# Sixteen-chunk FFN kernel: all hidden sums kept (29 batches in DRAM, three on chip) in place of two recomputed batches, with two sets of accumulator banks

## The reference

```
x  = x + layernorm(x) * scan(ctx*ctx)        # r = 0.9*r + kv_t over the tokens
z  = layernorm(x)
zq = clip(round(z/s1), 0, 255)*s1            # s1 = max of z over ALL batches / 255
h  = relu(zq @ w1q.T + b1q)                  # w1q: int8 per row, 2048 hidden features
hq = clip(round(h/s2), 0, 255)*s2            # s2 = max of h over ALL batches / 255
x  = x + hq @ w2q.T + b2q                    # w2q: int8 per row
```

## Time and profile before

| | us |
|---|---|
| median of 3 runs | 1323.02 |
| the profiled execution, its own time | 1323.59 |
| span of the profile | 1321.8 |
| stage A, to the first quantized x2 | 0 to 353 |
| stage B, first products | 359 to 832 |
| scales | 832 to 838 |
| stage C, second products | 839 to 1316 |
| last sums out and stored | 1316 to 1322 |

### The profile page before, as it was taken

How to read it: one execution, slowest core, us unless ns; L and a number is a source line. 1 busy time by engine, 2 the same in 40 slices (tenths; PEclk the granted TensorE clock), 3 DMA queues, 4 the chain that set the end, 5 groups by cost and what they waited for, 6 DMA issues and landing times.

```text
span 1321.8 us, 17311 instructions
## 1 busy us (share of the span) xinstructions
PE 1254.0 (95%) x5514; PEld 576.9 (44%) x5514; DVE 936.5 (71%) x1348; ACT 961.1 (73%) x1355; POOL 290.8 (22%) x777
## 2 busy tenths in 40 slices
PE   6778999999599999999999999899999999999998
PEld 3333444343344444444444444344444444444443
DVE  4979999999577777777777777664565555555565
ACT  5687878787677775777657776678878857888771
POOL 2859999999500000000000000000000000000000
PEclk9888999999799999999999999899999999999999
DMA  9887999997489996999969993799999999999973
GB/s 357 325 317 262 346 332 349 335 335 283 191 316 362 347 357 237 359 350 358 363 234 349 354 353 148 271 357 416 415 415 415 415 414 364 416 415 414 415 232 128
DMA packets 131521, 443.48 MB, mean 336 GB/s; under 512 B 10340, under 2 KB 10360, under 8 KB 118904
## 3 DMA queue, kind: packets, MB, share of 16 engines
q1 hardware_dynamic: 78648, 262.18, 50.8%
q10 hardware_dynamic: 52800, 180.37, 38.4%
HBM read 257.96 MB, written 184.55 MB: 335 GB/s over the span
## 4 chain that ended last, share of the span: by engine, by line
PE 66%; POOL 17%; DMA 6%; issue 4%; DVE 4%; ACT 2%; POOLq 1%; SPq 0%; ACTq 0%; DVEq 0%
PE ps L887 35%; PE ps L944 26%; DMA out_dram<-work 4%; PE ps L912 2%; POOL rstd L448 2%; POOL pw L432 2%; PE ps L866 2%; POOL pw L434 2%; POOL pw L431 1%; DMA work<-x_scratch 1%; POOL pw L429 1%; POOL rstd L466 1%; POOL zrow L446 1%; POOL mean L427 1%; POOL pw L428 1%
## 5 line engine op out<-in xcount | busy, mean ns | idle before, releaser
L887 PE MATMUL ps<-xq,w1T 128*128 128x512 f16 x2176 | 482.2, 381 | 1.4 <-DVE xq L748 1.4
L944 PE MATMUL ps<-w2T,xq 128*128 128x512 f16 x1984 | 438.8, 381 | 5.9 <-DVE work L790 3.2
L620 ACT ACTIVATE xq<-xq,hb,hs 128x512 f16<-128x512 f32 x480 | 355.7, 804 | 104.1 <-PE ps L944 93.3
L739 DVE TENSOR_REDUCE work<-xq 128x2 f32<-128x1024 f32 x240 | 292.8, 1220 | 122.1 <-ACT xq L566 122.1
L566 ACT ACTIVATE xq<-ps 128x1024 f32<-128x1024 f32 x240 | 245.8, 1024 | 135.5 <-PE ps L887 135.2
L887 PEld LDWEIGHTS ps<-xq,w1T 128*128 128x128 f16 x2176 | 212.2, 98 | 252.9 <-issue 3.6
L866 PE MATMUL ps<-xq,work 128*128 128x512 f32 x640 | 290.7, 612 | 31.6 <-ACT xq L499 21.2
L944 PEld LDWEIGHTS ps<-w2T,xq 128*128 128x128 f16 x1984 | 193.6, 98 | 246.1 <-DVE work L790 7.2
L866 PEld LDWEIGHTS ps<-xq,work 128*128 128x128 f32 x640 | 122.6, 195 | 197.4 <-issue 147.2
L790 DVE TENSOR_TENSOR work<-ps,cs_bc 128x512 f32<-128x512 f32 x128 | 87.9, 690 | 51.6 <-PE ps L944 44.8
L499 ACT ACTIVATE xq<-ps,rstd 128x512 f32<-128x512 f32 x128 | 77.9, 689 | 62.7 <-POOL rstd L466 56.1
(11 more groups left out here) (107 smaller groups left out, 639.6 us busy)
## 6 DMA issues: line engine op xcount, KB each, us to landing
hidden_scratch<-xq SPq DMA_DIRECT2D x224, 512.0 KB, 5.8
xq<-hidden_scratch ACTq DMA_DIRECT2D x224, 512.0 KB, 10.3
work<-x_scratch SPq DMA_DIRECT2D x33, 1024.0 KB, 7.9
xq<-in_x_dram SPq DMA_DIRECT2D x32, 1024.0 KB, 8.2
x_scratch<-xq SPq DMA_DIRECT2D x32, 1024.0 KB, 5.8
xq<-in_ctx_dram ACTq DMA_DIRECT2D x31, 1024.0 KB, 5.6
out_dram<-work SPq DMA_DIRECT2D x31, 1024.0 KB, 14.7
work<-x_scratch ACTq DMA_DIRECT2D x29, 1024.0 KB, 7.2
```

What stands on the lines that cost most here:

```text
L620: act.activation(hq[c % HQ], src[:, c % 2, :], ACT.Relu, bias=hb[:, q:q + 1], scale=hs[:, q:q + 1]).then_inc(h_scaled, 1)
L739: dve.tensor_reduce(hmax[:, b * NF + 2 * q:b * NF + 2 * q + 2], src, AX.X, ALU.max).then_inc(done, 1)
L887: last = pe.matmul(bank, w1T[:, k, f * P:(f + 1) * P], xq_rows(b, k), start=(k == 0), stop=(k == KD - 1))
L944: last = pe.matmul(acc_bank(i), src[:, i * P:(i + 1) * P], w2T[:, q, :], start=first, stop=final)
```

## The change

- `RECOMPUTED` goes away. Turns are the held batches, then the stored ones. Batches 9 and 20 are copied and have their maximum taken from the copy like all others. One of the two adds to the stored batches (29), one to the held ones (`HELD = 3`).
- `NKEEP` is 6 instead of 8. The places for hidden sums on chip are 30: 6 store buffers and 24 of the held batches; all 30 take loads in stage C.
- The first loads (6, not 8) are issued by SP, as soon as the last store has landed and the last stored pair has its maximum, while PE still makes the held batches. Before, ACT issued them after the last copy.
- Two sets of four accumulator banks, used by turns: 0, 1, 6, 7 and 2, 3, 4, 5. PE waits for `scale_out` of turn s-2.
- Slots of x2 follow from the three batches that are kept there from stage B on; the order store, load, store is the same.

```diff
-RECOMPUTED = (9, 20)
-HELD = 2
+HELD = 3
 NXQ = 3
-NKEEP = 8
+NKEEP = 6
...
+        def out_slot(s):
+
+            return (NB - HELD + s) % 3
...
+        def acc_bank(s, i):
+            return ps[:, ((0, 1, 6, 7), (2, 3, 4, 5))[s % 2][i], :]
...
             def load_x2c(s):
-                sp.wait_ge(out_stored[s % 3], 16 * (s // 3))
-                sp.dma_start(x2c[s % 3].rearrange("p i d -> p (i d)"), x2_dram[turns_c[s]]).then_inc(x2c_loaded[s % 3], 16)
+                if stores_until(s) > 1:
+                    sp.wait_ge(out_stored[out_slot(s)], 16 * (stores_until(s) - 1))
+                else:
+                    sp.wait_ge(x_scaled, (NB - 2) * NI)
+                sp.dma_start(x2c[out_slot(s)].rearrange("p i d -> p (i d)"), x2_dram[turns_c[s]]).then_inc(x2c_loaded[out_slot(s)], 16)
...
+            for n in range(NKEEP):
+                sp.wait_ge(h_stored[n], 16 * stores_in(n))
+            sp.wait_ge(kept_maxed, NLOAD)
+            for c in range(NKEEP):
+                sp.dma_start(hload[c].rearrange("p n t -> p (n t)"), h_dram[c // NP2, c % NP2]).then_inc(h_loaded[c], 16)
...
             def load_kept(c):
-                if c < NKEEP:
-                    act.wait_ge(kept_maxed, NLOAD)
-                else:
-                    act.wait_ge(h_scaled, 2 * (c - NKEEP + 2 + 1))
+                act.wait_ge(h_scaled, 2 * (c - NKEEP + 1))
...
-            for c in range(NKEEP):
-                load_kept(c)
...
-            def round_fresh(g, f):
-                if f >= 8 and g == 0:
-                    dve.wait_ge(h_scaled, 4)
...
-            def fresh_chunk(g, f):
-                c = g * NF + f
...
                 if first:
-                    wait_count(pe, acc_read, (s - 1) * NI + i + 1)
-                src = fresh_hq[q] if fresh else hq[ring_chunk(s, q) % HQ]
-                last = pe.matmul(acc_bank(i), src[:, i * P:(i + 1) * P], w2T[:, q, :], start=first, stop=final)
+                    wait_count(pe, acc_read, (s - 2) * NI + i + 1)
+                if (s, i, q) == (1, 0, 0):
+                    pe.wait_ge(out_scales, 1)
+                src = hq[(s * NF + q) % HQ]
+                last = pe.matmul(acc_bank(s, i), src[:, i * P:(i + 1) * P], w2T[:, q, :], start=first, stop=final)
```

More of the change, by code:

```diff
@@ L69, in build @@
     held = list(range(NB - HELD, NB))
-    stored = [b for b in range(NB) if b not in held and b not in RECOMPUTED]
-    passing = [b for b in range(NB) if b not in RECOMPUTED]
+    stored = list(range(NB - HELD))
     copied = stored + held
-    per_group = len(stored) // len(RECOMPUTED)
+    turns_c = held + stored
     NLOAD = len(stored) * NP2
[L75 to L88, removed]
     def xq_slot(b):
-        if b in RECOMPUTED:
-            return NXQ + RECOMPUTED.index(b)
-        return passing.index(b) % NXQ
+        return b % NXQ
     def copy_index(b, q):
         return copied.index(b) * NP2 + q
-    direct = [(b, q) for b in range(NB) for q in range(NP2) if b in RECOMPUTED]
     assert D == BANK and S == BANK and NI == KD == 4 and NB % XS == 0
@@ L186, in build @@
         PAIR = 2 * S
[L187 to L192, removed]
+        o = NXQ * KD * S // 2
+        places = [arena[:, at:at + PAIR] for at in range(o, o + 29 * PAIR, PAIR)] + [work[:, 3 * ROW + ROW // 2:4 * ROW]]
+        places = [a.rearrange("p (n t) -> p n t", n=2) for a in places]
+        assert NKEEP + HELD * NP2 == len(places)
+        hkeep = places[:NKEEP]
+        hheld = places[NKEEP:]
+        hload = places
         NRING = len(hload)
         hq = [xq[:, n * S:(n + 1) * S] for n in range(HQ)]
[L195 to L198, removed]
         decay_mat = work[:, 4 * ROW:4 * ROW + S]
@@ L303, in xq_rows, with stores_in, loads_until, stores_until @@
             return xq[:, at:at + S]
[L305 to L323, removed]
+        def stores_in(n):
+            return len(range(n, NLOAD, NKEEP))
+        def out_slot(s):
+            return (NB - HELD + s) % 3
+        def loads_until(s):
+            return len([m for m in range(HELD, s + 1) if out_slot(m) == out_slot(s)])
+        def stores_until(s):
+            return len([m for m in range(s + 1) if out_slot(m) == out_slot(s)])
+        def acc_bank(s, i):
+            return ps[:, ((0, 1, 6, 7), (2, 3, 4, 5))[s % 2][i], :]
         def all_stored_here(eng, done):
@@ L391, in _ @@
                 sp.wait_ge(out_ready, last * NI + i + 1)
-                sp.dma_start(out_rows[turns_c[last], :, i, :], x2c[last % 3][:, i, :]).then_inc(tail_stored, 16)
+                sp.dma_start(out_rows[turns_c[last], :, i, :], x2c[out_slot(last)][:, i, :]).then_inc(tail_stored, 16)
             sp.wait_ge(tail_stored, 16 * NI)
             for n in range(3):
-                sp.wait_ge(out_stored[n], 16 * len([m for m in range(last) if m % 3 == n]))
+                sp.wait_ge(out_stored[n], 16 * len([m for m in range(last) if out_slot(m) == n]))
         @block.gpsimd
@@ L620, in _ @@
                 act.activation(hq[c % HQ], src[:, c % 2, :], ACT.Relu, bias=hb[:, q:q + 1], scale=hs[:, q:q + 1]).then_inc(h_scaled, 1)
-                if c % 2 == 1 and NKEEP <= pair + 5 < NLOAD:
-                    load_kept(pair + 5)
+                if c % 2 == 1 and NKEEP <= pair + NKEEP - 1 < NLOAD:
+                    load_kept(pair + NKEEP - 1)
         @block.vector
@@ L890, in pair_free @@
             def pair_free(b, q):
[L892 to L895 removed]
+                pe.wait_ge(h_copied, copy_index(b, q) + 1)
             def hidden(b, q):
@@ L920, in _ @@
                     hidden(b, q)
[L923 to L931 removed]
             def second_product(s, i, q):
                 first, final = q == 0, q == NF - 1
[L935 removed]
                 if i == 0:
[L937 to L940 removed]
+                    pe.wait_ge(h_scaled, s * NF + q + 1)
                 if first:
[L942 to L944 removed]
+                    wait_count(pe, acc_read, (s - 2) * NI + i + 1)
[3 more added lines that the diff above has]
+                last = pe.matmul(acc_bank(s, i), src[:, i * P:(i + 1) * P], w2T[:, q, :], start=first, stop=final)
                 if final:
                     last.then_inc(acc_ready, 1)
[L947 removed]
+                elif i == NI - 1:
                     last.then_inc(hq_used, 1)
[L950 to L951 removed]
             spread(2)
@@ L957, in _ @@
                         second_product(s, i, q)
-                g, f, many = fresh_in.get(s, (0, 0, 0))
                 for q in range(EDGE, NF - EDGE):
```

84 lines of the change are left out of this document (17 added, 67 removed).

## The result

The changed kernel takes 1315.11 us (median of 5 runs, 1311.62 to 1315.69) against 1323.02 before (5 runs, 1321.09 to 1323.32): ratio 0.9934, 95% interval 0.9918 to 0.9951. It is faster by 0.66%. The time lies in the predicted range (1293 to 1316), but at its upper end, 7 us above the predicted 1308: the gain is 8 us where 15 were forecast. The profiled execution took 1312.24 us, with a span of 1310.4; it is one of the faster of the five, so 3 of the 7 us are scatter that the profile doesn't show.

What follows compares the result with a forecast made beforehand. PE bounds stages B and C, SP's order of store and load comes next. Span 1321.8 less 29.6 gives 1292.2 for PE by itself; SP's 15.64 us cycle raises it to 1307, and 1.2 more gives 1308; range 1293 to 1316.

Steps and rivals of the forecast that it cites:

- Removed matmuls: Recomputing's 128 matmuls, 27.6 us, leave PE's path; 3.5 us lay between stages B and C, so 24.2 were paid.
- turn 1: Stage C's second turn on PE took 16.3 us instead of 13.8; with two bank sets 2.5 us come back.
- the clock: PE's granted clock, half after the longer idle gap between stages B and C: costs 0, at most 3 us.
- PE alone: Sum with PE's stage C turns at 13.81 us: PE ends at 1286.5, span 1292.2, 29.6 less than before.
- Stage B: Six store buffers allow a store 9.2 us before ACT waits; the longest took 8.7; cost taken as 0.
- SP's chain: Stage C: store lands, then x2 load and next store; 15.64 us a cycle paces PE from turn 22, span 1307.
- First loads by SP: Moving the first hidden loads from ACT to SP, 3 MB before stage C, gains and costs nothing.
- the start of SP's chain: Early stage C: stores 1 and 2 take 12.3 to 13.6 us, under a turn; SP is behind from store 4, at 919.5.
- SP's cycle is a matter of its share of the engines: about a third: Stage C: beside ACT's backlog of hidden loads, SP's 2 MB a turn gets a third of the DMA engines, 15.64 us.
- ACT's full queue: Stage C, 16 hidden loads outstanding: ACT stands at its issue, paced at 14.9 us a turn; counted within the forecast.
- PE alone decides: Rival, chance 0.13: another division of the DMA engines gives SP a 10.1 us cycle in stage C; time 1293.
- The small terms at the end: Last turn of stage C: load 31 lands at 1298, its biases at 1300.6, 2 us more at the end.

Runs made afterwards that it cites:

- that lock opened alone: The changed kernel with all hidden loads of stage C issued by GpSimd instead of ACT (the first six instead of SP): 1312.66 us.
- Two experiments: Two edits to the changed kernel in stage C: each x2 load one turn later, behind the store, 1318.15 us; x2 loads issued by GpSimd, 1317.09 us.
- opening both: The changed kernel with three issuers in stage C, SP for hidden loads, GpSimd for x2 loads, ACT for output stores: 1295.62 us.

## Why the prediction was right, and where not

*Right, by its steps.* Removed matmuls, turn 1 and the clock give PE alone, 1292.2 in span: measured as 1292.4 without x2 loads. Stage B costs nothing; its longest store took 9.1 us where 9.2 were allowed, and five buffers showed that the limit lies further off than I had it. PE runs from turn 0 into turn 1 without a gap. SP's chain sets the end, with a cycle of 15.66 us where 15.64 was forecast, and 9.0 after the last hidden load where 9.5 was. First loads by SP: nothing, as said.

*Right by the range, with little to spare.* The forecast was that PE saves 29.6 us and SP's chain leaves 15 of them. It left 8. That the time fell into the range (to 1316) is due to its width as much as to the sum. One term that was too small is the start of SP's chain (two more, at the end, follow below). I let stores 1 and 2 land within a turn, as before the change. They took longer; these are the two stores issued between 875 and 891:

```profile
DMA to landing us min/median/max: 14.6/14.8/15.1
```

So SP was behind from store 2 on, not from store 4, and store 4 was 2.2 us later than I had it. Why these two took longer than before no run shows.

*Right in size only.* "SP's cycle is a matter of its share of the engines: about a third" was the wrong reading of a right number. With the store no longer behind the landing of the store before, the same queue moved its 2 MB in 13.8 us beside ACT's backlog. The rule of the Trainium skill that was weighed there (DMA: Bandwidth & Descriptors, queues, rings and completion order: round robin between queue rows, a packet at a time) can't be read as a fixed division, neither equal nor one to two: what a queue gets also depends on how much stands in it. In SP's order one or two of its transfers are under way, and it moves 2.1 million bytes in 15.66 us, 134 GB/s of the 415; with its order turned round there are up to three, and it moves them in 13.82 us, 152 GB/s. That much these runs show; how the engines divide between two queues that are never empty no run here isolates.

*What was read wrongly* is ACT's full queue. The sentence was "PE waits earlier, the end is the same". For the changed kernel it held: PE waits for ACT first, at 15.0 us a turn (14.9 was forecast), and with that lock opened alone the time is the same (1312.66 against 1315.11 and 1313.91). Three things beside it did not. The queue fills at 11 loads, not 16, so at 1016 instead of near 1150. PE's turns are long from 1079 on and not from turn 22, near 1150. "PE waits for scale_out, not for ACT" was wrong: it waits for both. And the rival *PE alone decides* said that another division of the engines would give 1293. Two experiments gave the stores their 13.8 us, until ACT's queue was full, and came to 1318 and 1317: a full queue is a bound of its own, which the prediction had only underneath SP's chain. It ties ACT, and through it PE, to the pace of the engines (15.15 us a turn), although a load is issued 50 us ahead of its use and was never older than 25 us when it landed. In the changed kernel the two locks overlap: opening ACT's alone changes nothing that is clear of the scatter, opening SP's alone loses 2 to 4 us, and opening both gains 18 to 19.5.

*The small terms at the end.* I had load 31's bias delay the end by 2 us; DVE was in time (its last add_bias began at 1300.9, its next scale_out at 1302.3), because PE came 4 us later than I had it, at 1304.8. Of these 4, 2.6 come from the later stores (25 and 26), 1.1 from the load of turn 27, which took 9.0 us instead of 7.9, and the rest from small waits in turn 29. The span is 1310.4 against 1307. The other 3 to 4 us up to the median are the scatter between the profiled run and the median (2.9) and the step from a span to its time (1.8, where I had taken 1.2).

## What to carry to other kernels

When a stage is full on the engine and on the transfers at once, look for what couples them: a program that waits for a landing before it issues the next transfer, and a compute engine that issues its own loads and stands when its queue is full. Open all of these at once, since here one alone showed nothing or a loss. And work that looks wasted (here recomputing) may be what keeps the transfers below such a limit, so a change that removes it should come with the numbers of the next limit.

## What the hardware showed that I had not expected

- ACT's queue accepted only so many transfers: with 11 loads of 512 KB (128 rows of 4 KB each) under way, the next issue took up to 4.8 us instead of 0.33 and stopped the issuing engine's program. SP's queue showed the same with hidden loads, GpSimd's did not with up to 15. Whether transfers, rows or bytes are counted no run here separates; at the very start SP's issue was long behind four larger ones.
- Moving the full queue to an engine with nothing else to do was worth 21.5 us, with the same transfers and the engines as full.
- The same traffic issued by SP (hidden loads), GpSimd (x2) and ACT (stores) ran at 417 GB/s beside a PE that was full to 1268.
